# A DLRM tower in steps of 256 samples: ten tables looked up a step ahead, one product matmul per sample, gathers held back only by room for rows

## The chip, the cores and the metric

The kernel runs on one core of a Trainium2 chip. The metric is device time in microseconds (us) of one execution, here the median of three runs. The engines are TensorE (PE; its weight loads are counted apart as PEld), VectorE (DVE), ScalarE (ACT), GpSimd (POOL) and SyncE (SP), which only issues DMAs.

## The reference

2048 samples each have a dense vector of 128 numbers and 26 ids, one for each embedding table (1000 to 125,000 rows of 128 float32). The 27 vectors of a sample (dense and 26 looked-up rows) are multiplied with one another, the 351 products above the diagonal go with the dense vector (twice) into a network of three layers:

```python
e = jnp.stack([tbl_0[ids[:, 0]], tbl_1[ids[:, 1]], ..., tbl_25[ids[:, 25]]], axis=1)
combined = jnp.concatenate([dense_features[:, None, :], e], axis=1)            # 2048 x 27 x 128
interactions = jnp.einsum('bfd,bgd->bfg', combined, combined)
z = jnp.concatenate([dense_features, interactions[:, _TRIU_I, _TRIU_J]], axis=1)  # 128 + 351
h = jnp.concatenate([z, r_dense_features], axis=1)                             # 607
h = jnp.maximum(h @ W_top1 + b_top1, 0.0)                                      # 512
h = jnp.maximum(h @ W_top2 + b_top2, 0.0)                                      # 256
y = h @ W_top3                                                                 # 1
```

## The kernel before

The 2048 samples are worked in 8 halves of 256, each of two tiles of 128. The vectors must lie in SBUF with their 128 numbers down the partitions (the array `XT`, one for even and one for odd halves, 32 places for the 27 vectors of a sample), and they come there in two ways.

*Gathered.* For 20 of the tables GpSimd issues an indirect DMA (L321) per table and tile, 320 in all, which fetches 128 rows into `rows`, samples down the partitions. TensorE transposes them (L400) in six groups, up to four vectors to a PSUM bank, and ACT copies the bank into `XT` (L585). `rows` has room for two tiles, so the gathers of a tile wait until all transposes two tiles back are done (`filled_rows`).

*Looked up.* Six tables of 1000 rows (`LOOKUP_TABLES`) lie in SBUF, split into a higher and a lower float32r part. TensorE spreads the ids of a table over the partitions of a PSUM bank (L361), DVE compares them with the row numbers, which gives a one-hot matrix of 8 blocks (L705), and TensorE multiplies the 8 blocks with both parts of the table (L372, 16 matmuls). ACT copies the result into `XT` (L574). The one-hots lie in two buffers.

*Products.* For every four samples one matmul (L415) multiplies the 128 columns of four samples with their 4 x 26 columns; the blocks off the diagonal are waste. A step of eight such matmuls fills two banks of `gram`; DVE (L785, L786) and ACT (L591, L592) copy the four diagonal blocks into `A`. A half has eight steps. When `A` is full, TensorE turns it (`unblock`, L429), ACT packs the 351 products per sample (L606), and TensorE turns these (`pairs`, L442) to be the first layer's input.

*Layers.* Inputs and weights are split in two float32r parts each, and a product is three matmuls (L453); DVE makes the lower parts of the inputs (L756 to L775). The last layer is plain float32 (L476).

All results but the products' go through a ring of three PSUM banks, in one order that `stages(kind)` writes out for all engines. The layers of a half are spread over the product steps of the next. The program is a start (START), three loops over four tiles (`Fori`, with registers in the waits), and an end (LAST, END). SP loads dense rows and ids by tile.

Of the kernel before, what the change touches and what calls it, by code (L numbers as in the profile page):

```python
# [12 lines left out]
P = 128  # L30
LOOKUP_TABLES = [2, 5, 10, 12, 13, 14]


def build(nc, aps, out):
# [4 lines left out]
    F = NTAB + 1  # L39
    H1 = aps["W_top1"].shape[1]  # L40
# [4 lines left out]
    HALF = 2 * TILE  # L45
    ROUND = 2 * HALF
    NROUND = B // ROUND - 1
# [6 lines left out]
    assert all(aps[f"tbl_{f}"].shape[0] == VP * KT for f in LOOKUP_TABLES)  # L54

    QUAD = 4
    NI = HALF // QUAD
    QW = 32
    NA = F - 1
    GROUPS_STEP = 8  # L60
    STEPS = NI // GROUPS_STEP
    PER_BANK = 4
    K_PAIR = [(k, min(P, PAIRS - k)) for k in range(0, PAIRS, P)]
    NB1 = 1 + len(K_PAIR)
    assert H1 // P == NB1
    T_BANKS = 5

    COUPLES_OF = [range(NA // 2 * b // T_BANKS, NA // 2 * (b + 1) // T_BANKS) for b in range(T_BANKS)]
    PAIR0 = [F * a - a * (a + 1) // 2 for a in range(F)]

    FEAT = [0] + [f + 1 for f in GATHER_TABLES]
    XGROUPS = [[0]] + [list(range(g, min(g + 4, len(FEAT)))) for g in range(1, len(FEAT), 4)]

    RING = 3
    USES_X = len(XGROUPS)
    USES_MLP = T_BANKS + len(K_PAIR) + H1 // P + H2 // P + 1

    USES_START = NTILE // 4 + 1 + NL + USES_X + 2 * USES_X + NL
    USES_ROUND = 4 * USES_X + 2 * NL + 2 * USES_MLP
    assert USES_ROUND % RING == 0 and NL <= STEPS and B % ROUND == 0 and NTILE % 4 == 0  # L80

    NRAW = 2
    SPLIT_ORDER = [*range(NRAW, NL), *range(NRAW)]
    EARLY_ROWS_OF = [range(0)] * (NL - 2) + [range(USES_X // 2), range(USES_X // 2, USES_X)]

    WARM_UP = 16


    START, WHOLE, LAST, END = range(4)
    TILES = {START: (2, 3), WHOLE: (0, 1, 2, 3), LAST: (0, 1)}  # L90

    PIECES = {1: ("layer1", 0), 2: ("layer1", 1), 3: ("layer1", 2), 4: ("layer1", 3),
              5: ("layer2", 0), 6: ("layer2", 1), 7: ("layer3", 0)}
    assert [n for layer, n in PIECES.values()] == [*range(H1 // P), *range(H2 // P), 0] and max(PIECES) < STEPS
    LOOKUP_AFTER = {START: {s: s for s in range(NL)}, WHOLE: dict(zip((0, 2, 3, 5, 6, 7), range(NL))), LAST: {}}
    assert len(LOOKUP_AFTER[WHOLE]) == NL
    RING_STAGES = ("rows", "lookup", "unblock", "pairs", "layer1", "layer2", "layer3")

    def stages(kind):

        if kind == END:
            yield "dense", 1, 0
            for b in range(T_BANKS):
                yield "unblock", 1, b
            for k in range(len(K_PAIR)):
                yield "pairs", 1, k
            for layer, n in PIECES.values():
                yield layer, 1, n
            return
        for t in TILES[kind]:  # L110
            h, q = divmod(t, 2)
            if q == 0 and kind != START:
                yield "dense", h, 0
            if q == 0 and kind != LAST:
                yield "spread", h, 0
            if q == 0 and kind != START:
                for b in range(T_BANKS):
                    yield "unblock", h, b
            if q == 1 and kind == START:
                yield "leftovers", h, 0  # L120
            for s in range(q * STEPS // 2, (q + 1) * STEPS // 2):
                piece = [(PIECES[s][0], h, PIECES[s][1])] if s in PIECES and kind != START else []
                yield "products", h, s
                if s == STEPS - 1:
                    yield from piece
# [712 lines left out]
```

## Time and profile before

| | |
|---|---|
| median of 3 runs | 785.9 us (785.33 to 788.93) |
| the profiled execution's span | 791.1 us |
| TensorE matmul / weight load busy | 62% / 54% |
| ACT busy | 33% |
| DVE busy | 29% |
| GpSimd busy | 39% |
| moved by DMA | 27.57 MB, 35 GB/s on the mean |
| chain that ended last | PE 42%, unknown releaser 22%, issue 20%, ACT 12%, DVE 3% |

The profiled execution took 791.1 us, 5.2 us more than the median; durations below are from it. A float32 matmul that isn't a transpose stands in the trace as two matmuls with a weight load each (L415: 512 in the program, x1024 here). "issue" is idle time in which the engine waits for nothing that the profile shows, "remote" is a wait whose releaser it doesn't know. PEclk is the granted TensorE clock, 1.00 being 2.4 GHz and 0.50 being 1.2 GHz.

### The profile page before, as it was taken

The numbers are of one execution on the slowest core, as the hardware profiler recorded it, in microseconds if no ns is written. First come the engines' busy times: TensorE is split into PE (matmuls) and PEld (weight loads), VectorE is DVE, ScalarE is ACT, GpSimd is POOL, SyncE is SP. The second block draws the span as 40 slices with busy tenths as digits, with TensorE's granted clock in tenths as the row PEclk, the third lists the DMA queues.
The fourth block names the chain that finished last, engine by engine and source line by source line (L and its number), as shares of the span: only waits on it lengthen the run. The fifth ranks groups of instructions, "written<-read, shape, count | busy, mean of one in ns | idle before, by whom it ended". The sixth has DMA issues, their size and how long they took to land.

```text
span 791.1 us, 8476 instructions
## 1 busy us (share of the span) xinstructions
PE 487.2 (62%) x3016; PEld 424.6 (54%) x3016; DVE 226.9 (29%) x296; ACT 262.0 (33%) x632; POOL 305.1 (39%) x327
## 2 busy tenths in 40 slices
PE   6407566526748086580956719476393855939977
PEld 4306556426637085470855518464282745827866
DVE  3207251222313142321413213133131332313231
ACT  1115131512416033160522615025150432405762
POOL 6751707370442606336072541705327071350000
PEclk8757767666959679596886959768596866958997
DMA  5620202110110101111010110101101020010000
GB/s 128 198 72 11 54 7 55 28 52 9 34 37 19 53 1 45 27 24 46 0 50 20 35 35 9 52 10 40 30 17 50 3 53 17 27 43 1 1 1 0
DMA packets 20003, 27.57 MB, mean 35 GB/s; under 512 B 10940, under 2 KB 13508, under 8 KB 19985
## 3 DMA queue, kind: packets, MB, share of 16 engines
q0 software_dynamic: 10240, 20.99, 10.3%
q1 hardware_dynamic: 9728, 6.32, 2.9%
q8 instruction: 12, 0.20, 0.1%
q14 instruction: 7, 0.05, 0.0%
q10 hardware_dynamic: 16, 0.01, 0.0%
HBM read 27.29 MB, written 0.01 MB: 35 GB/s over the span
## 4 chain that ended last, share of the span: by engine, by line
PE 42%; another core or an unknown queue 22%; issue 20%; ACT 12%; DVE 3%; DMA 0%; ACTq 0%; SPq 0%; DVEq 0%
PE gram L415 16%; PE ring L453 12%; PE ring L372 11%; ACT xt L585 6%; ACT pairs_or_h L606 4%; DVE onehot L705 2%; PE idb L361 1%; PE ring L442 1%; PE ring L476 1%; ACT xt L574 1%; ACT A L592 1%; DMA pairs_t_or_h<-in_ids 0%; DVE A L786 0%; DVE x_or_h_split L772 0%
## 5 line engine op out<-in xcount | busy, mean ns | idle before, releaser
L321 POOL DMA_INDIRECT rows<-in_tbl,ids_tile x320 | 304.3, 951 | 401.6 <-PE ring L400 306.7
L415 PE MATMUL gram<-xt 128*128 128x104 f32 x1024 | 161.4, 318 | 31.6 <-issue 28.3
L415 PEld LDWEIGHTS gram<-xt 128*128 128x128 f32 x1024 | 153.1, 233 | 38.5 <-issue 33.6
L372 PE MATMUL ring<-onehot,table_hi 125*128 125x256 f32 x368 | 113.1, 334 | 37.6 <-DVE onehot L705 31.3
L705 DVE TENSOR_TENSOR onehot<-idb,vrow 125x2048 fp32r<-125x2048 f32 x48 | 110.0, 2292 | 59.8 <-remote 47.2
L453 PE MATMUL ring<-x_or_h_split,w_hi 128*128 128x256 f32 (+1 forms) x384 | 95.6, 322 | 47.9 <-issue 40.2
L785 DVE COPY A<-gram 32x208 f32<-32x208 f32 x64 | 32.2, 503 | 309.6 <-remote 171.3
L591 ACT COPY A<-gram 32x208 f32<-32x208 f32 x64 | 32.4, 506 | 244.4 <-remote 163.9
L453 PEld LDWEIGHTS ring<-x_or_h_split,w_hi 128*128 128x128 f32 (+1 forms) x384 | 74.1, 219 | 64.0 <-issue 56.8
L372 PEld LDWEIGHTS ring<-onehot,table_hi 125*128 125x128 f32 x368 | 79.9, 217 | 48.0 <-issue 40.2
L372 PE MATMUL ring<-onehot,table_lo 125*128 125x256 f32 x368 | 103.7, 308 | 1.4 <-issue 1.4
L574 ACT COPY xt<-ring 128x256 f32<-128x256 f32 x48 | 29.1, 606 | 193.5 <-remote 132.2
L442 PE MATMUL ring<-ident,pairs_or_h 64*128 64x64 f32 (+1 forms) x96 | 12.2, 277 | 117.7 <-ACT xt L574 115.0
L453 PE MATMUL ring<-x_or_h_split,w_lo 128*128 128x256 f32 x192 | 59.7, 311 | 35.0 <-issue 35.0
L372 PEld LDWEIGHTS ring<-onehot,table_lo 125*128 125x128 f32 x368 | 80.8, 220 | 0.6 <-issue 0.6
L585 ACT COPY xt<-ring 128x256 f32<-128x256 f32 (+2 forms) x128 | 78.0, 787 | 0.1
L442 PEld LDWEIGHTS ring<-ident,pairs_or_h 64*128 64x128 f32 (+1 forms) x96 | 10.1, 183 | 119.6 <-issue 118.8
L453 PEld LDWEIGHTS ring<-x_or_h_split,w_lo 128*128 128x128 f32 x192 | 42.4, 221 | 29.0 <-issue 29.0
L400 PE MATMUL ring<-ident,rows 128*128 128x128 f32 x336 | 50.4, 285 | 6.5 <-ACT xt L585 4.1
L400 PEld LDWEIGHTS ring<-ident,rows 128*128 128x128 f32 x336 | 37.6, 144 | 17.1 <-ACT xt L585 11.6
L606 ACT COPY pairs_or_h<-ring 64x104 f32<-64x104 f32 (+12 forms) x208 | 42.3, 203 | 3.0 <-PE ring L429 0.3
L764 DVE TENSOR_TENSOR x_or_h_split<-pairs_t_or_h,x_or_h_split 128x256 fp32r<-128x256 f32 (+1 forms) x24 | 10.2, 424 | 89.2 <-ACT pairs_t_or_h L616 87.9
(46 smaller groups left out, 272.9 us busy)
## 6 DMA issues: line engine op xcount, KB each, us to landing
rows<-in_tbl,ids_tile POOLq DMA_INDIRECT x320
xt<-in_tbl SPq DMA_DIRECT2D x6, 500.0 KB
rows<-in_r_dense_features SPq DMA_DIRECT2D x16, 64.0 KB
A<-in_W_top SPq DMA_DIRECT2D x2, 256.0 KB
xt<-in_W_top SPq DMA_DIRECT2D x2, 256.0 KB
pairs_or_h<-in_W_top SPq DMA_DIRECT2D x1, 512.0 KB
ids_tile<-in_ids SPq DMA_DIRECT2D x16, 13.0 KB
pairs_t_or_h<-in_ids SPq DMA_DIRECT2D x1, 208.0 KB
```

The source lines that it names most:

```text
L321: pool.indirect_dma_start(rows[:, t % 2, 1 + r, :], None, aps[f"tbl_{f}"], bass.IndirectOffsetOnAxis(ap=ids_tile[:, t, f:f + 1].bitcast(U3 ...
L372: last = pe.matmul(ps[:, 0:HALF], part[:, m, k, :], onehot[:, buf, k, :], start=(k == 0 and part is table_hi), stop=(k == KT - 1 and part ...
L400: last = pe.transpose(ps[:, i * P:(i + 1) * P], rows[:, q, row, :], ident[:])
L415: last = pe.matmul(gram[:, s % 2, g // PER_BANK, col:col + QUAD * NA], four, cols, start=True, stop=True)
L442: last = pe.transpose(ps[0:w, j * NI:(j + 1) * NI], pairs[:, j, k0:k0 + w], ident[0:NI, 0:NI])
L453: last = pe.matmul(ps, w[wp][0:rows, k], x[xp][0:rows, k, :], start=(i == 0), stop=(i == len(terms) - 1))
L574: act.copy(XT[h][:, :, LOOKUP_TABLES[m] + 1], bank(start)[:, 0:HALF]).then_inc(emptied, 1)
L585: last = act.copy(xt[:, :, f0:f0 + step * (n - 1) + 1:step].rearrange("d s f -> d f s"), ps[:, i * P:(i + n) * P].rearrange("d (f s) -> d ...
L591: act.copy(*product_views(s, 2))
L606: last = act.copy(pairs[:, :, PAIR0[a]:PAIR0[a] + n], blk[:, :, a + 1:F])
L705: dve.tensor_tensor(onehot[:, buf], idb[0:VP, 0:HALF].unsqueeze(1).to_broadcast([VP, KT, HALF]), vrow[:].unsqueeze(2).to_broadcast([VP, KT ...
L785: dve.tensor_copy(*product_views(s, 0))
```

## The change

The kernel has no loops with registers any more: `stages()` lists all eight steps of 256 samples, and every engine's program is written out. In detail:

- Ten tables are looked up and 16 gathered (256 gathers). Lookups are made for the step that comes next, the table's ids arrive by a DMA that SP issues (broadcast to 128 partitions, 128 KB) and ACT copies them to PSUM (L525). One-hots are made in halves of 4 blocks, in three places. Four of the tables' lower parts are made by GpSimd (L322) among the first gathers, the rest by DVE.
- `rows` has 45 places, taken in turn. A gather waits only for the transposes of the bank in which the row 45 gathers back was; the last 20 places hold the ids of the first step's ten lookups at first, so their first gathers wait for `idb_ready`.
- `XT` has 27 places per sample and two steps. One matmul per sample (L419) loads 27 columns, streams 26 and writes to a quarter of the output partitions, 64 of them to each of the four groups of products in a step.
- The layers are plain float32 (L453 and L455, L464, L473): no splits of inputs or weights.
- The ring has four banks with a semaphore for each. DVE copies two of the ten groups of rows (L638) and half of `unblock` (L646), which ACT did.
- The host hands in the ids transposed as well, and W_top1 with its rows in the kernel's order of vectors.

```diff
-LOOKUP_TABLES = [2, 5, 10, 12, 13, 14]
+LOOKUP_TABLES = [2, 5, 10, 12, 13, 14, 15, 19, 23, 25]
+ROWS = 45
...
-        rows = sb("rows", [P, 2, 1 + NG, D])
-        XT = [sb(f"xt{h}", [D, HALF, QW]) for h in range(2)]
+        rows = sb("rows", [P, ROWS, D])
+        XT = sb("xt", [D, 2, BS, F])
...
             def products(n, s):
...
-                    four = XT[1 - h][:, s0:s0 + QUAD, :].rearrange("d j f -> d (j f)")
-                    cols = XT[1 - h][:, s0:s0 + QUAD, 0:NA]
-                    col = (g % PER_BANK) * QUAD * NA
-                    last = pe.matmul(gram[:, s % 2, g // PER_BANK, col:col + QUAD * NA], four, cols,
-                                     start=True, stop=True)
+                    for j in range(QUAD):
+                        sample = XT[:, n % 2, (s * GROUPS_STEP + g) * QUAD + j, :]
+                        last = pe.matmul(gram[QW * j:QW * j + F, s % 2, g * NA:(g + 1) * NA], sample, sample[:, 0:NA],
+                                         start=True, stop=True)
...
+            def gathers(k):
+                for g, f in enumerate(GATHER_TABLES):
+                    i = k * NG + g
+                    u, first = divmod(i - IDS0, IDS_ROWS)
+                    if 0 <= u < NL and first == 0:
+                        pool.wait_ge(idb_ready, u + 1)
+                    if i >= ROWS and (i == ROWS or bank_of(i - ROWS) != bank_of(i - ROWS - 1)):
+                        pool.wait_ge(ring_filled, filled("rows", *bank_of(i - ROWS)))
+                    pool.indirect_dma_start(
+                        rows[:, i % ROWS, :], None, aps[f"tbl_{f}"], ...
+                    ).then_inc(rows_landed[k % 3][g // GROUP], 16)
+                    if i in LO_BEHIND:
+                        lower_part(LO_BEHIND[i])
...
+            def spread_ids(u):
+                if u >= NL + IDS_SLOTS:
+                    sp.wait_ge(idb_ready, u - IDS_SLOTS + 1)
+                n, m = divmod(u, NL)
+                f = LOOKUP_TABLES[m]
+                src = aps["ids_t"][f:f + 1, n * BS:(n + 1) * BS].to_broadcast([P, BS])
+                sp.dma_start(ids_place(u), src).then_inc(...)
...
+            def layer1(n, b):
...
+                pe.matmul(ps, w1[:, 0, b * P:(b + 1) * P], x_dense[:, n % 2, :], start=True, stop=False)
+                for k, (k0, w) in enumerate(K_PAIR):
+                    last = pe.matmul(ps, w1[0:w, 1 + k, b * P:(b + 1) * P], x[0:w, k, :], start=False, stop=(k == KX - 1))
```

The order of a step, condensed from what `stages()` yields for all engines (n is the step, lookups are for step n + 1, layers of step n - 1):

```python
yield "products", n, 0, 0
yield from lookups(n + 1, 0); yield from layer("layer1", n - 1, 0)
yield from lookups(n + 1, 1); yield from layer("layer1", n - 1, 1); yield from lookups(n + 1, 2)
yield "products", n, 1, 0
yield from rows(n, 1, 0, 1); yield from layer("layer1", n - 1, 2); yield from lookups(n + 1, 3)
yield from rows(n, 1, 2, 3); yield from layer("layer1", n - 1, 3)
yield from rows(n, 1, 4); yield from lookups(n + 1, 4)
yield "products", n, 2, 0
yield from lookups(n + 1, 5); yield from layer("layer2", n - 1, 0)
yield from lookups(n + 1, 6); yield from layer("layer2", n - 1, 1)
yield "products", n, 3, 0
yield from lookups(n + 1, 7); yield from layer("layer3", n - 1, 0); yield from layer("unblock", n, 0, 1)
yield from rows(n + 1, 0, 0, 1); yield from lookups(n + 1, 8); yield from layer("unblock", n, 2, 3)
yield from rows(n + 1, 0, 2, 3, 4); yield from lookups(n + 1, 9); yield from layer("pairs", n, 0, 1, 2)
```

What stands in a row on TensorE before, in a whole half; `gram` is the products' PSUM, `ring` the ring:

```order
L415 MATMUL gram<-xt 128x104 [waits gram_dve,gram_act]
L415 MATMUL gram<-xt 128x104 x7
L372 MATMUL ring<-onehot,table_hi 128x256 [waits onehot_ready,emptied]
L372 MATMUL ring<-onehot,table_lo 128x256
```

And after, from the second products of a step on, where transposes of rows and a piece of the first layer (`x_dense`, `x`) stand between products and the next lookup:

```order
L419 MATMUL gram<-xt 27x26 [waits gram_dve,gram_act]
L419 MATMUL gram<-xt 27x26 x63
L400 MATMUL ring<-ident,dense 128x128 [waits ring_emptied1,rows_landed2_0,dense_landed1]
L400 MATMUL ring<-ident,rows 128x128 x3
L400 MATMUL ring<-ident,rows 128x128 [waits ring_emptied2]
L400 MATMUL ring<-ident,rows 128x128 x3
L453 MATMUL ring<-x_dense,w 128x256 [waits ring_emptied3]
L455 MATMUL ring<-x,w 128x256 x3
L379 MATMUL ring<-onehot,table_hi 128x256 [waits onehot_ready,ring_emptied0]
```

Eight wide product matmuls ahead of a lookup became 64 narrow ones, and a tile's first transposes no longer wait for all of its rows but for the first eight.

On GpSimd before, for two tiles in the loop:

```order
L317 ISA [waits filled_rows]
L321 DMA rows<-in_tbl,ids_tile 128x128 [waits ids_slot0]
L321 DMA rows<-in_tbl,ids_tile 128x128 x19
L328 ISA
L321 DMA rows<-in_tbl,ids_tile 128x128 [waits filled_rows,ids_slot1]
L321 DMA rows<-in_tbl,ids_tile 128x128 x19
```

And after, where the first 45 places have been taken once:

```order
L335 DMA rows<-in_tbl,ids_all 128x128 [waits idb_ready]
L335 DMA rows<-in_tbl,ids_all 128x128
L335 DMA rows<-in_tbl,ids_all 128x128 [waits ring_filled]
L335 DMA rows<-in_tbl,ids_all 128x128 x2
L335 DMA rows<-in_tbl,ids_all 128x128 [waits ring_filled]
L335 DMA rows<-in_tbl,ids_all 128x128 x3
```

One wait for 20 gathers became a wait for every three or four.

## Rows read from the trace of the kernel before

**Rows 1.** The page's part 1: busy us, share of the span, instructions.

```profile
PE 487.2 (62%) x3016; PEld 424.6 (54%) x3016; DVE 226.9 (29%) x296; ACT 262.0 (33%) x632; POOL 305.1 (39%) x327
```

**Rows 2.** Waits: who waits before what <- for whom: us, times, longest.

```profile
POOL rows L321 <- PE ring L400: 306.7, 14, 25.0
ACT xt L574 <- remote: 132.2, 11, 17.4
PE ring L442 <- ACT xt L574: 115.0, 6, 20.5
...
PE ring L453 <- issue: 75.2, 65, 2.5
```

**Rows 3.** Windows by half: us, then PE, PEld, DVE, ACT, POOL, PEclk, DMA share, GB/s.

```profile
0.00:76.30 76.30, 33.82 (x156) 27.30 (x156) 24.79 (x19) 19.20 (x29) 40.06 (x49) 0.71 0.39 104
166.30:262.70 96.40, 56.78 (x373) 49.39 (x373) 27.23 (x36) 31.46 (x78) 38.91 (x41) 0.77 0.11 30
645.00:742.00 97.00, 62.75 (x400) 55.50 (x400) 26.47 (x39) 34.33 (x86) 28.75 (x31) 0.75 0.08 22
742.00:791.10 49.10, 38.80 (x272) 34.31 (x270) 12.96 (x33) 24.47 (x65) 0.00 (x0) 0.89 0.00 1
```

**Rows 4.** Timeline around one burst: start, us, engine line op, [idle before <- releaser].

```profile
396.48 0.94 POOL L321 DMA_INDIRECT rows<-in_tbl,ids_tile  x1 [24.48 <-PE ring L400]
405.33 0.28 PE L372 MATMUL ring<-onehot,table_lo 125*128 125x256 f32 x1
420.28 0.95 POOL L321 DMA_INDIRECT rows<-in_tbl,ids_tile  x1 [0.30 <-issue]
424.88 0.51 ACT L591 COPY A<-gram 32x208 f32<-32x208 f32 x1 [19.28 <-remote]
```

**Rows 5.** Windows of 5 us, early and late in that burst.

```profile
400.00:405.00 5.00, 5.00 (x42) 4.74 (x41) 1.01 (x2) 1.02 (x2) 3.78 (x4) 1.00 0.21 52
410.00:415.00 5.00, 1.12 (x3) 0.86 (x3) 0.00 (x0) 0.00 (x0) 3.79 (x4) 0.50 0.18 52
```

**Rows 6.** Timeline of PE: layer 2 in the last half, without gathers.

```profile
756.87 0.35 PE L453 MATMUL ring<-x_or_h_split,w_hi 128*128 128x256 f32 x1
758.67 0.59 PE L415 MATMUL gram<-xt 128*128 128x104 f32 x4
```

**Rows 7.** Timeline: the other burst of that half.

```profile
441.82 0.95 POOL L321 DMA_INDIRECT rows<-in_tbl,ids_tile  x1 [20.59 <-PE ring L400]
451.35 0.70 PE L442 MATMUL ring<-ident,pairs_or_h 64*128 64x64 f32 x8
470.19 0.59 ACT L574 COPY xt<-ring 128x256 f32<-128x256 f32 x1 [17.38 <-remote]
```

**Rows 8.** Timeline of PE: matmuls in a row, for pitches.

```profile
401.20 1.93 PE L415 MATMUL gram<-xt 128*128 128x104 f32 x16
403.32 0.38 PE L361 MATMUL idb<-ids_t,ident_r 26*128 x1
404.09 0.28 PE L372 MATMUL ring<-onehot,table_lo 125*128 125x256 f32 x1
404.21 0.28 PE L372 MATMUL ring<-onehot,table_hi 125*128 125x256 f32 x1
434.43 1.02 PE L476 MATMUL ring<-pairs_t_or_h,w 128*1 128x256 f32 x4
440.26 0.66 PE L400 MATMUL ring<-ident,rows 128*128 128x128 f32 x4 [0.22 <-ACT xt L585]
```

**Rows 9.** The page's part 5: out<-in xcount | busy, mean ns | idle before.

```profile
L705 DVE TENSOR_TENSOR onehot<-idb,vrow 125x2048 fp32r<-125x2048 f32 x48 | 110.0, 2292 | 59.8 <-remote 47.2
L785 DVE COPY A<-gram 32x208 f32<-32x208 f32 x64 | 32.2, 503 | 309.6 <-remote 171.3
```

**Rows 10.** Timeline at the start: the 40th gather, the third lookup's copy.

```profile
52.72 0.95 POOL L321 DMA_INDIRECT rows<-in_tbl,ids_tile  x1 [0.30 <-issue]
60.06 0.60 ACT L574 COPY xt<-ring 128x256 f32<-128x256 f32 x1 [0.29 <-remote]
```

More of the change, by code:

```diff
@@ L137, in ring_start @@
[L137 to L157 removed]
+    XGROUPS = [list(range(g, min(g + 4, NG + 1))) for g in range(0, NG + 1, 4)]
@@ L159, in build @@
+    LO_ON_GPSIMD = sorted(LO_BEHIND.values())
+    LO_ON_VECTOR = [m for m in range(NL) if m not in LO_ON_GPSIMD]
     with ExitStack() as ctx:
@@ L364, in lookup @@
-            def lookup(start, buf, m, ready, col):
-                ps = claim(start)
-                pe.wait_ge(onehot_ready, ready)
-                for k in range(KT):
-                    for part in (table_hi, table_lo):
-                        last = pe.matmul(ps[:, 0:HALF], part[:, m, k, :], onehot[:, buf, k, :],
-                                         start=(k == 0 and part is table_hi), stop=(k == KT - 1 and part is table_lo))
-                    if k == 0 and m + 1 < NL:
-                        spread_ids(m + 1, col)
-                last.then_inc(looked_up, 1)
@@ L391, in transpose_rows, with claim, wait_emptied, lookup @@
-            def transpose_rows(r, start, t, g):
-                q = t % 2
+            def claim(*stage):
+                u = USE[stage]
+                if u >= RING:
+                    pe.wait_ge(ring_emptied[u % RING], u // RING)
+                return ring[:, u % RING, :]
+            def wait_emptied(*stage):
+                place, count = emptied(*stage)
+                pe.wait_ge(ring_emptied[place], count)
+            def lookup(n, m):
+                ps = claim("lookup", n, m, 0)[:, 0:BS]
+                u = n * NL + m
+                if n == 0:
+                    pe.wait_ge(*lo_ready(m))
+                for c in range(CH):
+                    pe.wait_ge(onehot_ready, CH * u + c + 1)
+                    for k in range(KC):
+                        for part in (table_hi, table_lo):
+                            last = pe.matmul(ps, part[:, m, c * KC + k, :], onehot[:, (CH * u + c) % SLOTS, k, :],
+                                             start=(c == 0 and k == 0 and part is table_hi),
+                                             stop=(c == CH - 1 and k == KC - 1 and part is table_lo))
+                    last.then_inc(chunk_used if c < CH - 1 else ring_filled, 1)
@@ new lines, in _ @@
+            act.wait_ge(const_ready, 3)
+            act.copy(x[:, 0, 0:P], ident[:])
+            act.wait_ge(pads_cleared, 1)
+            for m in (0, 1):
+                lay_out_ids(m)
+                upper_part(m)
+            for stage, n, a, b in stages():
+                if stage == "lookup":
+                    if n * NL + a + 2 < NB * NL:
+                        lay_out_ids(n * NL + a + 2)
+                    if n == 0 and a + 2 < NL:
+                        upper_part(a + 2)
+                    store_lookup(n, a)
+                elif stage == "rows" and not rows_on_vector(a, b):
+                    store_rows(n, a, b)
+                elif stage == "products":
+                    store_products(n, a)
+                elif stage == "unblock" and not unblock_on_vector(a):
+                    store_unblocked(n, a)
+                elif stage == "pairs":
+                    store_pairs(n, a)
+                elif stage == "layer1":
+                    store_layer(stage, n, a, h1, b1)
+                elif stage == "layer2":
+                    store_layer(stage, n, a, h2, b2)
+                elif stage == "layer3":
+                    store_y(n)
```

894 lines of the change are left out of this document (373 added, 521 removed).

## The prediction

> **What bounds the kernel now.** I read the page's busy shares first: no engine is busy throughout, TensorE 62%, GpSimd 39% [rows 1]. So the waits come next. GpSimd waits 306.7 us for the transposes L400, which make room for rows. TensorE, ACT and DVE each have long waits without a named partner: 115.0 us of TensorE before L442 in 6 pieces of up to 20.5 us, 132.2 us of ACT before L574, and TensorE's own "issue" before L453 [rows 2]. The stretches show a period: a half (256 samples) takes 94 to 97 us, six of them (742.0 - 166.3) / 6 = 95.95 us, and the last, with no gather in it, ends in 49.1 us [rows 3].
>
> Inside a half the timeline gives the reason. The 20 gathers of a tile run 1.25 us apart, from 396.48 to 420.28. TensorE works at full pace until its row at 405.33 ends, then shows only a few matmuls, and ACT's copy of the products that TensorE issued before that lookup starts only at 424.88, 3.7 us after the last gather left GpSimd [rows 4]. In 5 us TensorE has 42 matmuls before this and 3 in it, while its granted clock falls from 2.4 GHz (1.00) to 1.2 GHz (0.50) [rows 5]. The same twelve layer-2 matmuls, L453 right behind a lookup or products, run from 756.87 to 758.67 where no gather runs, and from about 407 to 425 where one does [rows 4, 6]. The other burst of the half starts at 441.82. TensorE issues until 452.1 (the eight transposes from 451.35), and ACT's copy of the lookup that stands ahead of these starts at 470.19, again when the gathers are through [rows 7]. No instruction named waits for data there. So in a burst of gathers TensorE gets through about 90 matmuls at its pace, some 10 us, and is then held until 3.7 us after the last gather's end. The half loses 424.9 - 405.6 = 19.3 us and, with the 17.38 us in ACT's row, 17.4 us, together 36.7 us. What holds it I can't tell from the trace. That it is tied to the gathers I take as shown, by all bursts.
>
> So the kernel alternates: gathers in lockstep with transposes, 16 times, and TensorE's work mostly between them. Both the gathers' number and TensorE's work count.
>
> **The change part by part, for a step of 256 samples.** Pitches are from one matmul to the next of one kind. A float32 matmul that isn't a transpose stands in the trace as two.
> - Gathers: 32 rather than 40. Each of the two bursts is 4 x 1.25 = 5 us shorter: -10.0 us. The order on GpSimd shows waits for room in fours and threes, but the five transposes groups of a tile stand within some 65 matmuls, fewer than the 90 that get through, so I count one burst of 20 us per tile. At the step's end a burst covers cheaper matmuls (narrow ones and transposes), so its 90 are worth 1.5 us less: +1.5.
> - Lookups: 10 tables rather than 6, each 16 matmuls 0.12 us apart [rows 8]: 4 x 16 x 0.12 = +7.7 us.
> - Products: 64 matmuls of 4 samples (128 in the trace) at (1.93 - 0.28) / 15 = 0.110 us [rows 8] (0.28 is the last one's own time, as in the lookup rows) are 14.1 us. Now 256 matmuls, 512 in the trace, of 27 loaded and 26 streamed columns. No row shows one so narrow. From below, 0.110 scaled by 27 / 128 columns gives 23 ns. From above, the smallest pitch in the trace, 64 streamed columns at L442, (0.70 - 0.28) / 7 = 60 ns [rows 7]. I take 35 ns, nearer the scaled one because it is the same operation with both its loads and its columns cut, with 12 ns for going to another quarter of the array each time, which no row shows: 17.9 us, +3.8.
> - By the Trainium skill ("TensorEngine Tiling (Array Packing)", Instruction Overhead) a matmul costs about 60 cycles however narrow it is. At 2.4 GHz that is an estimate of 25 ns; no row here shows it, and by it the sum would be 4096 x 10 ns = 41 us lower than mine.
> - Spreading ids: 6 matmuls of 0.38 us, partly beside the next [rows 8], go: I take -1.9 us; ids come by DMA broadcast on SP and an ACT copy into PSUM instead.
> - Layers: 84 split matmuls at 0.12 and 4 at 0.213 (L476, (1.02 - 0.38) / 3, its own time as L361's for as many columns) are 10.9 us; now 26 float32 matmuls, 52 in the trace, at 0.213 [rows 8]: 11.1 us, +0.2.
> - Transposes of rows: 34 for 42 at (0.66 - 0.28) / 3 = 0.127 [rows 8], -1.0.
> - Waits. The half is 95.95 - 36.7 = 59.2 us outside the holds; its matmuls by these pitches are some 46 us, so 13 us are slow clock and waits on ACT and DVE. The splits of x and h1 on DVE go, DVE takes part of the copies, the ring has four places. I take 5 us off (0 to 9 is possible).
> - DVE and ACT: 20 one-hot halves at half of 2.29 us, 16 copies like L785's of twice the size, 2 row copies and 13 small ones come to some 37 us on DVE; ACT has 10 id copies, 10 lookup copies at 0.60 [rows 10], 8 row copies, 8 of products and the layers', about 35 us [rows 9]. Both are below the step's time, so I cost them at nothing; the cover is TensorE's 63 us, and if products cost nothing it is still 45.
>
> The step: 95.95 - 10.0 + 1.5 + 7.7 + 3.8 - 1.9 + 0.2 - 1.0 - 5.0 = 91.25 us, of which 36.7 - 10.0 + 1.5 = 28.2 us is held by gathers; without them 63.05.
>
> The start: products began at 76.3 us [rows 3]. A first burst of 40 gathers ended at 53.7, the third lookup was stored from 60.06 on, and three more with the transposes took the 16 us until the products [rows 10]. Now 45 gathers and four subtractions on GpSimd come first (no row has one there; I put 1 to 3 us each): TensorE resumes near 72 with four lookups done, and six lookups and the transposes make 90 us (80 to 100).
>
> The sum. 256 - 45 = 211 gathers are 6.6 steps' worth: 6.6 x 91.25 = 602.3. Another 0.4 step at 63.05 is 25.2. The last looks nothing up: 63.05 - 10 x 1.92 = 43.9. The first has no layers to run: -11. Start 90, the last step's layers 18 (the end of the last half is such work now, I take a third of its 49.1 us [rows 3]). Together 768.4 us of span. The profiled span was 791.1 where the runs' median is 785.9; taking off the same 5.2 gives **763 us**, 3% less.
>
> **Rivals.**
> A, the hold goes. What speaks for it: the program has no loops with registers now, and what holds TensorE is not named. Against: the bursts of the part ahead of the loops hold it too. Then 8 x 63.05 - 19.2 - 11 + 18 and a start of 70 give 562, less 5: 557 us.
>
> B, slower: a narrow matmul has a floor. Place: products, 4096 entries after the change. At the smallest pitch that the trace has, 60 ns, the price is 4096 x 25 ns = 102 us: 865 us. It decides from (785.9 - 763) / 4096 = 6 ns more on, so from 41 ns. For it: a pitch under 60 isn't in the trace at all. Against: that one has 64 columns streamed and 128 loaded. The Trainium skill ("TensorE: Matmul & The Clock Gate", Wait — 56ns, not 53.3ns?) has a rule that ends here: with hardware decode off, the sequencer needs about 62 ns per matmul. By that figure the estimate is 763 + 4096 x 27 ns = 874; the trace's 60 ns agrees with it as far as it goes, but can't tell it from the price of 64 columns.
>
> C, slower by the new transfers: 67 broadcasts of ids, 128 KB each, now run between the bursts too. At the start, with tables and weights on the DMA queues beside the gathers, ACT's second and third lookup copies came only at 59.2 and 60.06, over 5 us after the last gather's end at 53.67 [rows 10], where elsewhere it is 3.7. If each broadcast holds it about 1 us (an estimate: no row prices one; those 2 us more for the last few transfers are nearest), 67 us come on top: 830. Against: dense rows and ids load between bursts before and TensorE runs at pace.
>
> **How the numbers follow.** My forecast 0.42, with its own range 720 to 805 (pitch 27 to 43 ns, start, waits). A 0.18, B 0.22, C 0.18. The range 590 to 885 leaves out two thirds of A, 0.12, and the upper parts of B and C, 0.08. About 0.5% is what a measurement can tell from no change. Faster: 0.33 of mine, A's 0.18, 0.03 of C: 0.54. Same 0.07, from mine and C. Slower 0.39.
>
> **What the profile after would show.** Right: bursts of 16 gathers 20 us long, with TensorE near idle from its ninetieth matmul or so until 3 to 4 us after the last; about 13 of them; steps of 88 to 94 us between first products; 64 products with 128 entries in 4.5 us. Wrong, A: no idle stretch of TensorE during gathers, GpSimd's waits over 100 us still there. B: entries of the products 60 ns or more apart. C: TensorE's gaps where SP's broadcasts run and no gather does. DVE or ACT above 80% would show that I took the bound from the wrong engine. A start over 100 us would show that the tables or the ids gate it.

## The result, and the profile after

The changed kernel takes **649.0 us** (median of 4 runs, 647.1 to 652.7) beside 786.2 us for the kernel before: ratio 0.826, 95% interval 0.8225 to 0.8295. Forecast were 763 us, range 590 to 885. The direction was right, the gain six times what I forecast: 137 us, not 23.

The page's busy shares, as in [rows 1]:

```profile
PE 402.7 (62%) x6280; PEld 356.5 (55%) x6280; DVE 297.4 (46%) x361; ACT 257.0 (40%) x492; POOL 256.4 (40%) x267
```

TensorE's share is what it was, with twice the records, and DVE and ACT stay under 50%. Waits, as in [rows 2]:

```profile
POOL rows L335 <- PE ring L400: 238.0, 13, 20.0
DVE A L630 <- PE gram L419: 163.0, 32, 55.7
PEld gram L419 <- issue: 136.6, 110, 4.4
PE gram L419 <- issue: 122.1, 103, 4.2
DVE onehot L622 <- remote: 121.7, 11, 13.5
ACT xt L529 <- remote: 118.9, 11, 12.0
```

Windows by step, answering to [rows 3]: two of the five whole steps, then the last but one and the last.

```profile
404.18:480.02 75.84, 48.79 (x783) 43.35 (x784) 35.52 (x44) 30.55 (x61) 30.21 (x32) 0.82 0.19 48
480.02:557.75 77.73, 50.42 (x784) 45.16 (x784) 35.55 (x44) 30.94 (x61) 30.20 (x32) 0.79 0.18 47
557.75:603.10 45.35, 44.19 (x783) 40.45 (x784) 32.98 (x42) 30.06 (x60) 2.83 (x3) 0.96 0.10 22
603.10:646.40 43.30, 33.99 (x659) 27.14 (x658) 12.03 (x24) 20.34 (x44) 0.00 (x0) 1.00 0.01 2
```

A whole step takes 75 to 78 us where I had 91.25. The two that have next to no gathers take 45 and 43. So the alternation is still there, and the timeline shows it, as [rows 4] and [rows 7] did: first the two bursts of 16 gathers in one step (first and last gather of the first, first and last of the second), then TensorE around both. Below, an entry is one matmul's row in the trace, and a hold is a stretch in a burst of gathers in which TensorE starts next to nothing.

```profile
380.82 0.94 POOL L335 DMA_INDIRECT rows<-in_tbl,ids_all  x1 [19.55 <-PE ring L400]
...
399.56 0.94 POOL L335 DMA_INDIRECT rows<-in_tbl,ids_all  x1 [0.30 <-issue]
...
418.06 0.94 POOL L335 DMA_INDIRECT rows<-in_tbl,ids_all  x1 [17.55 <-PE ring L400]
...
436.79 0.94 POOL L335 DMA_INDIRECT rows<-in_tbl,ids_all  x1 [0.30 <-issue]
```

```profile
404.18 1.71 PE L419 MATMUL gram<-xt 128*27 128x26 f32 x128 [11.42 <-ACT xt L529]
...
415.93 1.27 PE L419 MATMUL gram<-xt 128*27 128x26 f32 x128
417.13 0.33 PE L400 MATMUL ring<-ident,dense 128*128 128x128 f32 x1
...
428.89 0.31 PE L419 MATMUL gram<-xt 128*27 128x26 f32 x16 [2.39 <-issue]
...
432.24 0.20 PE L419 MATMUL gram<-xt 128*27 128x26 f32 x1 [1.22 <-issue]
...
439.27 0.25 PE L419 MATMUL gram<-xt 128*27 128x26 f32 x2 [1.20 <-issue]
...
440.67 1.43 PE L419 MATMUL gram<-xt 128*27 128x26 f32 x100 [0.46 <-issue]
```

The reader is to see three things. TensorE starts again at 404.18, 3.7 us after the last gather's end at 400.50, as before, and at 440.67, 2.9 us after the second burst's. A stage of products that falls into the hold starts with 16 entries, then goes at one or two every 0.7 to 1.4 us, and the 100 that are left go in 1.4 us once it ends. And outside a hold the 64 products of a stage, 128 entries, take 417.13 - 415.93 = 1.20 us with the step to the next matmul, 9.4 ns each (8.5 from the first entry to the last). The forecast had 35.

The first of these two holds has the releaser ACT L529, which copies the last lookup, and that copy itself starts late:

```profile
388.50 0.28 PE L379 MATMUL ring<-onehot,table_lo 125*128 125x256 f32 x1
...
403.46 0.66 ACT L529 COPY xt<-ring 128x256 f32<-128x256 f32 x1 [11.02 <-remote]
```

The lookup's last matmul stands in the trace at 388.50, and ACT gets to copy its result 15 us later. So a hold delays also what follows on matmuls whose rows are already there; whether the matmul or only the signal of its end is late, the trace doesn't show.

### The profile page after: what moved, and what is told of

Read it like the earlier page. It is cut to its first block, busy times and chain, and to the rows that moved or that the text cites. A ratio compares the mean times of both kernels' runs of the same rounds, so it can differ in the third digit from the quotient of the medians.

```text
span 646.4 us, 14206 instructions
## 1 busy us (share of the span) xinstructions
PE 402.7 (62%) x6280; PEld 356.5 (55%) x6280; DVE 297.4 (46%) x361; ACT 257.0 (40%) x492; POOL 256.4 (40%) x267
## 4 chain that ended last, share of the span: by engine, by line
PE 53%; issue 22%; another core or an unknown queue 11%; ACT 9%; POOL 1%; DMA 1%; DVE 1%; SPq 1%; ACTq 0%; DVEq 0%
PE ring L379 24%; PE gram L419 10%; PE ring L455 6%; PE ring L464 4%; PE ring L400 4%; ACT xt L537 3%; PE ring L453 2%; ACT pairs_and_more L549 2%; PE ring L442 1%; ACT xt L529 1%; DMA w<-in_tbl 1%; PE ring L473 1%; POOL rows L335 1%; POOL table_lo L322 1%
## 5 line engine op out<-in xcount | busy, mean ns | idle before, releaser
L335 POOL DMA_INDIRECT rows<-in_tbl,ids_all x256 | 246.2, 962 | 314.3 <-PE ring L400 238.0
L622 DVE TENSOR_TENSOR onehot<-idb,vrow 125x1024 fp32r<-125x1024 f32 x160 | 189.3, 1220 | 145.8 <-remote 121.7
L379 PE MATMUL ring<-onehot,table_hi 125*128 125x256 f32 x640 | 185.9, 322 | 23.6 <-issue 6.3
L419 PE MATMUL gram<-xt 128*27 128x26 f32 x4096 | 66.3, 203 | 192.0 <-issue 122.1
L379 PE MATMUL ring<-onehot,table_lo 125*128 125x256 f32 x640 | 174.4, 304 | 0.0
L419 PEld LDWEIGHTS gram<-xt 128*27 128x27 f32 x4096 | 53.2, 117 | 208.0 <-issue 136.6
L379 PEld LDWEIGHTS ring<-onehot,table_hi 125*128 125x128 f32 x640 | 137.1, 214 | 30.7 <-issue 14.8
L379 PEld LDWEIGHTS ring<-onehot,table_lo 125*128 125x128 f32 x640 | 137.6, 215 | 0.6
L529 ACT COPY xt<-ring 128x256 f32<-128x256 f32 x80 | 54.0, 675 | 180.7 <-remote 118.9
L630 DVE COPY A<-gram 27x416 f32<-27x416 f32 x32 | 28.1, 878 | 163.0 <-PE gram L419 163.0
L537 ACT COPY xt<-ring 128x512 f32<-128x512 f32 (+1 forms) x64 | 61.5, 1030 | 24.4 <-PE ring L442 8.7
L543 ACT COPY A<-gram 27x416 f32<-27x416 f32 x32 | 28.2, 882 | 98.2 <-PE gram L419 98.2
L455 PE MATMUL ring<-x,w 128*128 128x256 f32 (+1 forms) x192 | 46.7, 379 | 0.0
L455 PEld LDWEIGHTS ring<-x,w 128*128 128x128 f32 (+1 forms) x192 | 36.7, 191 | 5.2
L464 PE MATMUL ring<-h,w 128*128 128x256 f32 x128 | 31.2, 388 | 1.0 <-ACT h L559 1.0
L525 ACT CAST idb<-ids_spread 128x256 f32<-128x256 int32 x70 | 31.5, 451 | 0.0
L631 DVE COPY A<-gram 27x416 f32<-27x416 f32 x32 | 28.2, 883 | 0.4
L544 ACT COPY A<-gram 27x416 f32<-27x416 f32 x32 | 28.3, 883 | 0.4
L464 PEld LDWEIGHTS ring<-h,w 128*128 128x128 f32 x128 | 23.9, 196 | 4.6 <-ACT h L559 1.8
```

Source lines behind the costliest of these rows:

```text
L335: pool.indirect_dma_start(rows[:, i % ROWS, :], None, aps[f"tbl_{f}"], bass.IndirectOffsetOnAxis(ap=ids_all[:, k, f:f + 1].bitcast(U32), a ...
L379: last = pe.matmul(ps, part[:, m, c * KC + k, :], onehot[:, (CH * u + c) % SLOTS, k, :], start=(c == 0 and k == 0 and part is table_hi), s ...
L419: last = pe.matmul(gram[QW * j:QW * j + F, s % 2, g * NA:(g + 1) * NA], sample, sample[:, 0:NA], start=True, stop=True)
L455: last = pe.matmul(ps, w1[0:w, 1 + k, b * P:(b + 1) * P], x[0:w, k, :], start=False, stop=(k == KX - 1))
L464: last = pe.matmul(ps[:, 0:BS], w2[:, k, b * P:(b + 1) * P], h1[:, k, :], start=(k == 0), stop=(k == H1 // P - 1))
L525: act.copy(idb[:, u % 2, 0:BS], ids_place(u)).then_inc(idb_ready, 1)
```

## Where the 122 us between the sum and the span are

The span is 646.4 us, the sum of the forecast was 768.4.

| | forecast | measured |
|---|---|---|
| start and first step, to the second step's first products | 90 + 80.3 | 175.2 |
| five whole steps | 456.3 | 382.6 |
| the next | 80.0 | 45.4 |
| the last, and its layers | 61.9 | 43.3 |

Of a whole step's 91.25 - 76.5 = 14.7 us, products are 17.9 - 4.8 = 13.1 (four stages of 1.20 us against four of 4.5). The holds are 11.4 and some 14.2 us (426.5 to 440.67), 25.6 where I had 28.2; all other terms together came out 1 us longer than I had them, and I haven't read them one by one. The last but one step is shorter by the same 13, and by a second thing: 61 gathers and not 45 ran in one go at the start (the first of the next burst is at 117.61), so 12 bursts were left, six steps' worth and not 6.6, which is 0.6 x 28.2 = 17 us of hold less.

Eight steps' products, 105 us, and these 17 make up the 122, but not because the rest was right: the start with the first step took 4.9 us more than forecast although its products too were shorter, so 18 us are missing there, and the later steps were 18 us shorter beyond the two causes. The start's part is a hold as well: the first stage of products begins at 49.10, falls into the burst of 45 gathers from 39.88 to 97.58 and has its last 34 entries only at 104.36, 6.8 us after that burst. I had products begin at 90.

## Experiments, first set: the products, and the loops

A set is a group of runs made together, the kernel before among them each time. In this set it took 784.8 us.

**One narrow product matmul per sample in the kernel before.**

```diff
                 for g in range(GROUPS_STEP):
                     s0 = (s * GROUPS_STEP + g) * QUAD
-                    four = ...
-                    cols = ...
-                    col = (g % PER_BANK) * QUAD * NA
-                    last = pe.matmul(gram[:, s % 2, g // PER_BANK, col:col + QUAD * NA], four, cols, ...)
+                    for j in range(QUAD):
+                        sample = XT[1 - h][:, s0 + j, :]
+                        col = (g % PER_BANK) * QUAD * NA + NA * j
+                        last = pe.matmul(gram[QW * j:QW * (j + 1), s % 2, g // PER_BANK, col:col + NA], sample,
+                                         sample[:, 0:NA], start=True, stop=True)
```

> The kernel before with one product matmul per sample (32 columns loaded, 26 streamed, a quarter of the array each), all else as it was. Theory (the products' pitch is what I had wrong: 128 matmul entries took 1.08 us from first to last where the clock was full, 8.5 ns each and not 35): a half's products go from 14.1 us to about 5, so 8 halves lose up to 73 us, and somewhat less as far as the products stand inside a hold by the gathers: 715 to 745 us. Rival (the gain came from the ring, the splits and the waits, products were covered by DVE and ACT copies anyway): within 10 us of 786.

Measured: **804.9 us**, ratio 1.025 (1.0216 to 1.0279), and 806.0 in a later set. Both theories fell: slower. The timeline of this kernel's TensorE over a burst that starts at 406.61:

```profile
408.01 0.90 PE L415 MATMUL gram<-xt 128*32 128x26 f32 x44 [0.32 <-issue]
...
412.22 0.32 PE L415 MATMUL gram<-xt 128*32 128x26 f32 x4 [1.17 <-issue]
...
422.87 0.20 PE L415 MATMUL gram<-xt 128*32 128x26 f32 x1 [1.83 <-issue]
...
434.77 0.94 PE L415 MATMUL gram<-xt 128*32 128x26 f32 x50 [0.50 <-issue]
```

From the burst's first gather to the first long gap TensorE started 64 matmul entries in 4.3 us here, and 68 in 8.9 us in the kernel before (to the row at 405.33 [rows 4]). In the changed kernel's burst from 418.06 it is 57 in 8.2 us, and in the other burst of the kernel before, from 441.82 [rows 7], 52 in 9.5. So what a burst lets through is a count of entries, 50 to 70, and not a time. Narrow products use it up on work that is worth 0.5 us, and the hold starts over 4 us earlier, in both bursts. I take it that this eats the 9 us that a half's products got shorter, and more: its halves take 97.7 us (406.61 to 504.32) against 95.0 for the same stretch of the kernel before (396.48 to 491.51).

**One wide product matmul per four samples in the changed kernel.**

```diff
+                flat = XT[:, n % 2].rearrange("d s f -> d (s f)")
...
-                    for j in range(QUAD):
-                        sample = XT[:, n % 2, (s * GROUPS_STEP + g) * QUAD + j, :]
-                        last = pe.matmul(gram[QW * j:QW * j + F, s % 2, g * NA:(g + 1) * NA], sample, sample[:, 0:NA], ...)
+                    s0 = (s * GROUPS_STEP + g) * QUAD
+                    last = pe.matmul(gram[0:QUAD * F, s % 2, (g % 4) * QUAD * NA:(g % 4 + 1) * QUAD * NA],
+                                     flat[:, s0 * F:(s0 + QUAD) * F], XT[:, n % 2, s0:s0 + QUAD, 0:NA], ...)
```

> The changed kernel with one product matmul per four samples again (108 columns loaded, 104 streamed; its blocks don't lie where the copies read, so the products are not those of the reference; the work of every other engine is as before). Theory: a step's products go from 4.8 us to 64 x 2 x 0.110 = 14.1 us, less what lies in a hold: 700 to 723 us. Rival (products hidden by the holds and other waits): under 665 us.

The transposes that warm TensorE up at the start were spread over eight places in PSUM as well. Measured: **688.9 us**, ratio 0.878 (0.8759 to 0.8807): 40 us more than the changed kernel, between the two ranges. A stage outside a hold takes 3.0 us, not 1.2:

```profile
430.62 3.20 PE L419 MATMUL gram<-xt 128*108 128x104 f32 x32
433.66 0.27 PE L400 MATMUL ring<-ident,dense 128*128 128x128 f32 x1
```

A step here is 81.8 us ((498.12 - 170.75) / 4 between its steps' first products), 5.3 more than 76.5, where the lengths alone would give over 7. The stage that stands in the hold costs nothing extra here: in the five whole steps it takes 10.9 to 11.7 us from its first entry to the next matmul, with narrow products 10.7 to 13.1. So of the change's 137 us narrow products are 40 on such an occasion.

**The changed kernel, 16 matmuls in a row to one quarter.** The two loops over `g` and `j` are swapped.

> The changed kernel with the two loops over samples swapped: 16 matmuls in a row go to the same quarter, then 16 to the next, and so on. Theory (the 8.5 ns come from four quarters working at the same time): a stage of 128 entries gets slower, up to the scaled 23 ns of my lower bound each, 2.9 us rather than 1.2, so 32 stages cost up to 55 us more: 680 to 705 us. Rival (a narrow matmul is that short by itself): within 5 us of 649.

Measured: **714.0 us**, ratio 0.911 (0.9075 to 0.9135), and 712.0 in a later set: slower than wide products, and above the 680 to 705 of the theory that four quarters work at the same time. The row of a stage:

```profile
403.26 3.45 PE L419 MATMUL gram<-xt 128*27 128x26 f32 x128
406.64 0.39 PE L379 MATMUL ring<-onehot,table_hi 125*128 125x256 f32 x1
```

3.38 us for 128 entries, 26.4 ns each, is close to the 23 ns that scaling by columns gave as my lower bound. In turn over the four quarters the same matmuls take 9.4. Two stages of a step take longer than that: the first, behind a hold and at a granted clock of 0.51 (1.2 GHz), up to 5.6 us, and the one in the hold 14.0 to 16.1 where it was 10.7 to 13.1. So a longer stage in a hold is not free here, as it was with 32 wide entries. The Trainium skill ("TensorEngine Tiling (Array Packing)", Key Properties) says that different tiles can load weights and multiply in parallel; the factor of 2.8 agrees. The Trainium skill's other figure on that page (Instruction Overhead), about 60 cycles however narrow a matmul is, at 2.4 GHz an estimate of 25 ns, agrees with the run in one quarter, and it isn't a bound on matmuls that alternate.

**The kernel before, loops written out.** The five `Fori` became Python loops.

> The kernel before with its five loops over rounds written out, nothing else changed. Theory (loops cost little and have nothing to do with the hold by gathers): TensorE is still held until 3.6 to 3.8 us after each burst's last gather, time within 8 us of 786. Rival (waits against registers, or the loop's end, cost time; or the written out program starves TensorE of instructions): 20 us or more either way.

Measured: **765.6 us**, ratio 0.978 (0.9717 to 0.9835). The loops are worth 19 us (13 to 22 by the interval), which I had not costed; both expectations, within 8 us and 20 or more, were missed. A half goes from (623.95 - 242.32) / 4 = 95.4 us, in the later profile of the kernel before that is named below, to (603.70 - 240.89) / 4 = 90.7, measured between the last layers. The hold stays, as windows early and late in a burst show (columns as in [rows 5]), so it has nothing to do with loops or registers:

```profile
387.00:392.00 5.00, 5.00 (x42) 4.74 (x42) 2.52 (x8) 1.51 (x3) 3.78 (x5) 1.00 0.18 52
397.00:402.00 5.00, 1.91 (x6) 1.09 (x5) 0.69 (x2) 0.70 (x2) 3.78 (x5) 0.67 0.18 52
```

## Second set: the gathers, and a surprise

In this set of runs the kernel before took **489.7 us**. Below, an occasion is the time of one set, named by what the kernel before took then. Nothing had been changed in it. Over all seven sets of runs it took 785 to 786 us in three (the forecast's own is one, the first set above another) and 489 to 493 us in four; no set had both. Comparisons below are within a set only.

**The changed kernel, plain DMAs for gathers.** Each indirect DMA becomes one of the first 128 rows of the same table, so rows don't follow the ids.

```diff
-                    pool.indirect_dma_start(
-                        rows[:, i % ROWS, :], None, aps[f"tbl_{f}"],
-                        bass.IndirectOffsetOnAxis(ap=ids_all[:, k, f:f + 1].bitcast(U32), axis=0),
-                    ).then_inc(rows_landed[k % 3][g // GROUP], 16)
+                    pool.dma_start(rows[:, i % ROWS, :], aps[f"tbl_{f}"][0:P, :]).then_inc(
+                        rows_landed[k % 3][g // GROUP], 16)
```

> The changed kernel with each of the 256 indirect gathers replaced by a plain DMA of the first 128 rows of the same table from the same engine, with the same waits and bytes (so rows don't follow the ids). Theory (it is the indirect gathers' work on GpSimd and their descriptors that hold TensorE): the hold goes or gets much shorter, a step is 55 to 63 us: 520 to 580 us. Rival (any DMA traffic of this size between the queues holds it, or the gap is a wait for the rows' data): the gaps after a burst stay, 620 us or more.

**Gathers further apart.** Behind each but the first 42, GpSimd clears a buffer of 128 x 360 and waits for it; `rows` has 42 places and not 45.

> The changed kernel with a memset of 128 x 360 on GpSimd behind each gather after the first 42 (42 places for rows to make room for its target), so gathers run some 1.9 to 2.1 us apart rather than 1.25. Theory (TensorE gets a share of what the gathers take between two gathers): while gathers run it now keeps a good part of its pace and the hold per burst shrinks to under 5 us, though bursts are 30 us long: 600 to 640 us. Rival (a burst holds TensorE for as long as it lasts, from a fixed count of instructions on): bursts of 30 us hold it 20 us each: 720 to 760 us.

**Transposes of rows spread out.** In `stages()` the ten groups stand one by one, each behind products, a lookup or a layer, for instance:

```diff
             yield "products", n, 1, 0
-            yield from rows(n, 1, 0, 1)
             yield from layer("layer1", n - 1, 2)
+            yield from rows(n, 1, 3)
             yield from lookups(n + 1, 3)
-            yield from rows(n, 1, 2, 3)
             yield from layer("layer1", n - 1, 3)
             yield from rows(n, 1, 4)
```

> The changed kernel with the ten groups of transposes of a step put one by one between the other stages, in place of five in a row twice, so that gathers are let go three or four at a time. Theory (what holds TensorE is a burst that lasts longer than it takes to use up some 50 to 70 matmul instructions): gathers come in bursts of 4 to 5 us with pauses, no long hold is left: 560 to 620 us. Rival (the held time goes by the number of gathers, not by how they are bundled): within 10 us of 649.

Then the changed kernel itself:

> The changed kernel as it is, again, since in the last runs the kernel before took 490 us and not 785, and no trace there shows a hold of TensorE in bursts of gathers. Theory: the hold belongs to the occasion (the chip or what it was doing), not to the kernels. Where the kernel before takes some 490 us, this one has no hold either: its step is 76.5 us less two holds of about 11 and 13 us and the slow clock behind them, 50 us, so 8 steps and the start of 70 give about 430 us, ratio 0.86 to 0.90. Where the kernel before takes 785 us, 649 us again. Rival: the change itself keeps part of the hold, over 500 us beside 490.

| | us | ratio to before | again, in later sets |
|---|---|---|---|
| changed kernel | 420.7 | 0.858 (0.8522 to 0.8638) | |
| plain DMAs | 402.6 | 0.826 (0.8191 to 0.8336) | 403.0, 403.0 |
| gathers apart | 465.4 | 0.953 (0.9446 to 0.9623) | 465.2, 465.0 |
| rows spread | 423.4 | 0.871 (0.8622 to 0.8797) | 422.7, 422.8, 421.5 |

What was expected of the repeats, which were meant to fall on an occasion of 785 us and never did:

> The changed kernel with its ten groups of transposes of rows put one by one between the other stages, again, beside the changed kernel. Where the kernel before takes 785 us: theory (a burst holds TensorE once some 50 to 70 of its matmul instructions are through) 560 to 620 us; rival (the held time goes by the number of gathers) 640 to 660 us. Where it takes 490 us: 423 us again, 0 to 15 us below the changed kernel.

> The changed kernel with each indirect gather replaced by a plain DMA of the first 128 rows of the same table from GpSimd, again. Where the kernel before takes 785 us: theory (indirect gathers are what holds TensorE there) 400 to 480 us, no gap of 8 us or more on TensorE behind a burst; rival (any transfers do) over 600 us. Where it takes 490 us: 403 us again.

> The changed kernel with its ten groups of transposes of rows one by one between the other stages, once more, since the occasions of 785 and 490 us for the kernel before alternate. At 785 us: theory (a burst holds TensorE once some 50 to 70 of its matmul instructions are through) 560 to 620 us; rival (the held time goes by the number of gathers) 640 to 660 us. At 490 us: 423 us again.

> The changed kernel with plain DMAs of 128 rows in place of indirect gathers, once more. At 785 us: theory (indirect gathers hold TensorE) 400 to 480 us; rival (any transfers issued by GpSimd do) over 600 us. At 490 us: 403 us again.

> The changed kernel with gathers some 1.8 us apart rather than 1.25 and 42 places for rows, once more. At 785 us: theory (TensorE gets what is left between two gathers) 580 to 640 us; rival (a burst holds it for its whole length) 720 to 760 us. At 490 us: 465 us again.

> The changed kernel with its ten groups of transposes of rows one by one between the other stages, now in a set of runs without the kernel of plain DMAs, since the kernel before took 490 us in the three sets that had that one in them and 785 us in the three that had not. If it takes 785 us here: theory (a burst holds TensorE once some 50 to 70 of its matmul instructions are through) 560 to 620 us; rival (the held time goes by the number of gathers) 640 to 660 us. At 490 us: 423 us again, and the set has nothing to do with it.

> The changed kernel with gathers some 1.8 us apart, in a set of runs without the kernel of plain DMAs. If the kernel before takes 785 us here: theory (TensorE gets what is left between two gathers) 580 to 640 us; rival (a burst holds it for its whole length) 720 to 760 us. At 490 us: 465 us again.

The changed kernel on this occasion, its busy shares and a step in windows (columns as in [rows 3]):

```profile
PE 369.7 (89%) x6280; PEld 328.4 (79%) x6280; DVE 294.3 (71%) x361; ACT 256.6 (62%) x492; POOL 256.1 (61%) x267
```

```profile
137.95:185.14 47.19, 45.34 (x783) 40.26 (x783) 35.36 (x44) 30.65 (x61) 35.61 (x39) 1.00 0.33 85
```

Same instructions, same 783 matmul entries in a step, 47.2 us rather than 76.5, and a granted clock of 1.00 (2.4 GHz) in this step. Gathers run 1.25 us apart here too:

```profile
138.43 0.94 POOL L335 DMA_INDIRECT rows<-in_tbl,ids_all  x1 [0.30 <-issue]
139.68 0.95 POOL L335 DMA_INDIRECT rows<-in_tbl,ids_all  x1 [0.30 <-issue]
```

They run so without a pause, the last of 237 at 336.87, and TensorE has no hold beside them. So **gathers don't hold TensorE by themselves; something on some occasions does, while gathers run.** Between the two occasions a step differs by 29.3 us, of which 25.6 are the two holds; the clock in a step is 0.79 to 0.82 with them and 1.00 without. The start differs by 54.8 us: the first stage of products begins at 49.10 or 48.45 and ends at 105.0 or 50.25. Six steps and the start are 54.8 + 6 x 29.3 = 231 us, and the spans differ by 646.4 - 416.4 = 230.0. So the whole difference lies where the holds are, and the holds as read are 25.6 of each step's 29.3.

Gathers do cost a little where there is no hold. A stage of products beside them takes 199.22 - 197.47 = 1.75 us:

```profile
197.47 1.82 PE L419 MATMUL gram<-xt 128*27 128x26 f32 x128
199.22 0.33 PE L400 MATMUL ring<-ident,dense 128*128 128x128 f32 x1
```

Once the gathers are over it takes 1.20 again (338.29 to 339.49). And in the kernel of plain DMAs, with transfers of the same size running, it is 1.20 too:

```profile
150.86 1.27 PE L417 MATMUL gram<-xt 128*27 128x26 f32 x128
152.06 0.39 PE L377 MATMUL ring<-onehot,table_hi 125*128 125x256 f32 x1
```

Plain DMAs gain 18 us, and four stages of 0.55 us are some 2.2 us of a step's part in that; GpSimd is 145.2 us busy with them, not 256.1. Spacing (a gather every 1.63 us) makes GpSimd the bound: its gathers run without a pause until 424.82 of 465.3 us, and TensorE waits 38.4 us for their rows. Spreading the rows does nothing here (422.7 beside 420.7 in one set), since gathers don't come in bursts where there is no hold; what it does on an occasion of 785 us stays open. A guess that the kernel of plain DMAs in a set made the difference fell with the last set, which had 490.7 us without it. A guess of the same kind is not tested: the kernel with its rows spread was in all four sets with 490 us and in none of the three with 785. One chip against another isn't the answer: the first set of experiments, with 785 us, and two of the sets with 490 ran on the same chip.

The kernel before, again for its profile:

> The kernel before itself, for its profile where it takes some 490 us. Theory (the hold is all the difference between 785 and 490 us, with the slow clock that follows each): no gap on TensorE behind bursts, a half of 256 samples is 95.95 - 36.7 = 59 us less some 3 us of slow clock, so 55 to 58 us; granted clock over 0.9; GpSimd's 320 gathers at 1.25 us are 400 us of 490, the longest queue. Rival: something else is faster too (pitches of matmuls, copies on DVE and ACT, time from gather to gather).

It fell on 785.7 us, with the hold, so there is no trace of the kernel before at 490 us. In the same set the narrow products gave 806.0 us and the quarters 712.0, with these words ahead of them:

> The kernel before with one product matmul per sample. Where the kernel before takes 490 us: theory (narrow matmuls in turn over the quarters take 8.5 to 9 ns per entry, and lost in the other case only because they used up a burst's count of instructions sooner) a half's products go from 14.1 to 5 us: 425 to 450 us. Rival (GpSimd's gathers with their waits bound it, 14.1 us of products are cover): 475 to 495 us. Where it takes 785 us: 805 again.

> The changed kernel with 16 matmuls in a row to the same quarter. In the first such run entries stood 27 to 28 ns apart, 3.6 us for 128, where four quarters in turn gave 8.5 ns. Where the kernel before takes 490 us: theory (TensorE bounds it) 32 stages x 2.4 us = 77 us more: 480 to 505 us beside 421. Rival: under 450 us. Where it takes 785 us: 714 again.

## Why the prediction was wrong

- *What bounds the kernel*: right for the occasion, in its size too. Hold until 2.9 and 3.7 us after a burst (6.8 after the longest), 25.6 us per step (28.2 forecast), bursts of 16 gathers 20 us long. "That it is tied to the gathers I take as shown, by all bursts" is too much: they are its time, not its cause. The "about 90 matmuls" that a burst lets through were 68 and 52 by the rows of the two bursts. Between its two occasions the kernel before differs by 295 us.
- *"I take 35 ns, nearer the scaled one"*: this step failed. Measured are 9.4 ns, under my lower bound of 23. The bound was right for matmuls to one place (26.4), and I added 12 ns "for going to another quarter of the array each time", when it is going to another quarter that makes them overlap. The term was 13.1 us per step too high, 105 us in eight steps, of 122. The page of the Trainium skill that bears on it, "TensorEngine Tiling (Array Packing)", I had named, and used only its section Instruction Overhead.
- The runs qualify this. The pitch is the largest error of the sum, but undoing narrow products costs only 40 us, because three wide stages of a step are longer and the fourth stands in a hold. The other 97 of the 137 us must lie in the loops (19 us in the kernel before), in shorter and fewer bursts and in waits on copies; no run prices these in the changed kernel, so this split is argued and not shown.
- *"211 gathers are 6.6 steps' worth"*: 192 in 12 bursts and 3 at the end; 17 us.
- *The start, 90 us, and its sign "a start over 100 us would show that the tables or the ids gate it"*: the first stage ended at 105.0, and neither did. It was the hold of the first long burst; without it, on the other occasion, the stage ends at 50.25. That the start's error and those of the later steps cancel, 18 us each, is luck.
- *Rival A* (the hold goes): not in the forecast's runs. On the other occasion it did, for both kernels: 421 us, but beside 490, a ratio of 0.858. Its 557 us was too high, mostly by the same pitch.
- *Rival B* (a floor for narrow matmuls, 865 us): wrong, no floor of 60 ns; entries come 9.4 ns apart. But the first experiment shows another way for narrow matmuls to lose, which I did not think of: their number.
- *Rival C* (ids hold TensorE): wrong. Between bursts, 405.7 to 415.7, TensorE was busy 10.00 of 10.00 us with ids landing.
- Layers and lookups, and DVE and ACT at nothing: right as a whole within the 1 us a step that is left above. DVE at 46% was late once at the start, by 5.8 us (for the lower part of a table, L608).

What stays open is what holds TensorE on an occasion of 785 us. It comes in with the number of TensorE entries, while gathers run, and in every kernel that was run on such an occasion. Instructions that arrive late don't end it: the changed kernel's instruction queues (q8 and q14) move no packet from 392.8 to 404.1 nor from 426.5 to 440.6, in its two holds of a step, and q8 moves 49 packets on either occasion. The Trainium skill ("NOTIFIC — the notification-queue block", Overflow: three behaviours, one of which stalls the engine) describes records that instructions write to memory, and a mode in which a full queue stalls the engine that writes them. A count of entries could be used up in this way; no run here shows it, nor why it should happen while gathers run.

## What to carry to other kernels

Small matmuls with outputs in different quarters of the partitions should take turns over the quarters: 9.4 ns per entry in turn, 26.4 in a row. Price such a matmul from the overlap, not by scaling a full one's pitch. When an engine stops with no wait of its own, count what it issued before stopping as well as the time, and time the unchanged kernel on more than one occasion before building a forecast on it: here the largest term, 230 us, belonged to the occasion. This change was good on both (0.826 and 0.858); one that trades few instructions for many lost on one of them (1.025) and wasn't measured on the other.

## What was not expected of the hardware

- The same kernel took 785 or 490 us, and 649 or 421, with gathers at the same 1.25 us.
- With the hold, TensorE starts 50 to 70 matmul entries after a burst's first gather, in 4.3 us or in 8.9, and ACT's copy of a lookup comes 15 us behind the lookup's last row.
- A float32 matmul of 128 x 27 by 26 columns costs 2 x 9.4 ns in turn over the quarters and 2 x 26.4 in a row to one. A stage of 64 in turn takes 1.75 us rather than 1.20 when indirect gathers run beside it without a hold, and 1.20 beside plain DMAs of the same size.
